# Three PSUM slots for the score tiles of the first two heads, and a load semaphore of their own for queries and keys, in an attention stage

## What is computed

```
qkv = (h @ W_qkv + b_qkv).reshape(b, l, 3, H, D)
q, k, v = (qkv[:, :, 0], qkv[:, :, 1], qkv[:, :, 2])
scores = jnp.einsum('blhd,bmhd->bhlm', q * scale, k)
attn = jax.nn.softmax(scores, axis=-1)
o = jnp.einsum('bhlm,bmhd->blhd', attn, v).reshape(b, l, c)
```

## Time and profile before

| | us |
|---|---|
| median of 3 runs | 3302.26 (3299.76 to 3304.22) |
| the profiled execution | 3293.01 |
| its span from the first to the last instruction | 3291.3 |
| mean granted TensorE clock in it | 0.937 of full speed |
| PE busy in it | 2889.1 (88%) |
| DVE, POOL, ACT busy in it | 1710.2, 1524.9, 1399.2 |

### The profile page before, as it was taken

How to read it: one execution, slowest core, us unless ns; L and a number is a source line. 1 busy time by engine, 2 the same in 40 slices (tenths; PEclk the granted TensorE clock), 3 DMA queues, 4 the chain that set the end, 5 groups by cost and what they waited for, 6 DMA issues and landing times. The chain is left out here.

```text
span 3291.3 us, 49525 instructions
## 1 busy us (share of the span) xinstructions
PE 2889.1 (88%) x16066; PEld 2291.0 (70%) x16066; DVE 1710.2 (52%) x2926; ACT 1399.2 (43%) x1758; POOL 1524.9 (46%) x1144
## 2 busy tenths in 40 slices
PE   6759899967999999999999867649999999999976
PEld 2247777844666666666666556549999999999965
DVE  3446566546888888888888667831111111111125
ACT  2112222215888888898888812211111111111112
POOL 1232322115888888888888848842222222222210
PEclk9869899977999999999999978869999999999988
DMA  5365566561333333333333157567121121111144
GB/s 168 135 228 203 184 212 216 187 176 42 73 80 78 70 80 81 71 76 81 75 73 80 39 175 243 209 225 230 35 69 35 35 69 35 48 56 35 49 138 145
DMA packets 337308, 373.72 MB, mean 114 GB/s; under 512 B 166161, under 2 KB 229273, under 8 KB 337166
## 3 DMA queue, kind: packets, MB, share of 16 engines
q1 hardware_dynamic: 329688, 359.12, 36.7%
q10 hardware_dynamic: 7482, 12.69, 1.3%
HBM read 221.81 MB, written 149.36 MB: 113 GB/s over the span
## 5 line engine op out<-in xcount | busy, mean ns | idle before, releaser
L757 POOL TENSOR_TENSOR a_pl<-a_pf,a_ph 128x1024 fp32r<-128x1024 f32 x384 | 913.1, 2398 | 57.0 <-ACT a_pf L840 56.6
L774 DVE TENSOR_REDUCE a_mx<-a_psum_s 128x1 f32<-128x1024 f32 x512 | 626.0, 1223 | 203.2 <-PE a_psum_s L855 195.1
L838 ACT ACTIVATE a_ph<-a_psum_t 128x1024 fp32r<-128x1024 f32 x512 | 526.1, 1027 | 166.6 <-PE a_psum_t L870 148.0
L1424 POOL TENSOR_TENSOR m_al<-m_af,m_ah 128x256 fp32r<-128x256 f32 x288 | 212.5, 738 | 764.9 <-DVE m_ah L1433 764.9
L1472 PE MATMUL m_psum_h<-m_ht,m_w 128*128 128x256 f32 x4032 | 533.3, 283 | 33.6 <-DMA m_w<-w_s 25.0
L1472 PEld LDWEIGHTS m_psum_h<-m_ht,m_w 128*128 128x128 f32 x4032 | 507.4, 189 | 37.2 <-issue 37.1
L1433 DVE CAST m_ah<-m_af 128x256 fp32r<-128x256 f32 x288 | 84.6, 294 | 837.0 <-ACT m_af L1410 837.0
L1486 PE MATMUL m_psum_y<-m_w,m_ah 128*128 128x288 f32 x2304 | 504.4, 296 | 1.4 <-DVE m_y L1450 1.2
L1410 ACT ACTIVATE m_af<-m_psum_h,m_bias 128x256 f32<-128x256 f32 x288 | 137.3, 477 | 813.4 <-PE m_psum_h L1472 813.4
L887 PE MATMUL a_psum_o<-a_ph,a_vs 128*100 128x512 f32 x1024 | 406.6, 397 | 3.7 <-POOL a_pl L757 3.6
L888 PE MATMUL a_psum_o<-a_pl,a_vs 128*100 128x512 f32 x1024 | 403.9, 394 | 0.0
(11 more groups left out here) (215 smaller groups left out, 3184.8 us busy)
## 6 DMA issues: line engine op xcount, KB each, us to landing
a_qs<-q_s SPq DMA_DIRECT2D x192, 144.0 KB
a_ks<-k_s SPq DMA_DIRECT2D x192, 144.0 KB
w_s<-q_ws SPq DMA_DIRECT2D x64, 324.0 KB, 3.4
h_s<-p_ht SPq DMA_DIRECT2D x40, 512.0 KB, 5.3
m_ht<-h_s SPq DMA_DIRECT2D x16, 1280.0 KB, 8.1
v_s<-q_vo SPq DMA_DIRECT2D x64, 288.0 KB, 2.3
a_vs<-v_s SPq DMA_DIRECT2D x128, 144.0 KB
q_s<-q_qko SPq DMA_DIRECT2D x32, 512.0 KB, 2.7
```

Source lines behind the costliest of these rows:

```text
L757: pool.tensor_tensor(pl[:, s % RING], pf[:, s % RING], raw(ph[:, s % RING]), ALU.subtract).then_inc(lo_pool, 1)
L774: dve.tensor_reduce(mx[:, u % 2, t:t + 1], p_s[:], AX.X, ALU.max).then_inc(s_free, 1)
L838: act.activation(ph[:, s % RING], p_t[:, s % 2], ACT.Exp, scale=SCALE)
L1424: pool.tensor_tensor(al[:, f % RING], af[:, f % RING], raw(ah[:, f % RING]), ALU.subtract).then_inc(lo_ready, 1)
```

## The change

The lead's tiles go round three slots: `p_s` and the two halves of `p_t`, tile n to slot n % 3. PE waits before tile n (from n = 3 on) for the reduction of tile n-3, and no longer for that of tile n-1. The first two scores steps of head 0, which overwrite the halves of `p_t`, wait for the last reductions that read these (`s_free` at 14 and 15). DVE's `turn` of head 0 stands behind the ninth reduction, where it stood behind the eighth.

`loaded[u]` becomes `qk_in[u]` (six DMAs) and `v_in[u]` (two). Score tiles wait for `qk_in`, at the place where they waited for `loaded`. The value product of each head's first step waits for `v_in`, a wait that wasn't there, in all 64 heads. Nothing is computed in another way, and no DMA changes its place.

```diff
-    LOADS = 8
+    QK_LOADS, V_LOADS = 6, 2
+    LEAD = 2 * KT
...
+        lead_slots = (p_s[:], p_t[:, 0], p_t[:, 1])
...
-                                         t[s, bass.ds(hd * D, D), :]).then_inc(loaded[u], 16)
+                                         t[s, bass.ds(hd * D, D), :]).then_inc(qk_in[u], 16)
...
-                          .then_inc(loaded[u], 16)
+                          .then_inc(v_in[u], 16)
...
+                def lead_max(n):
+
+                    dve.wait_ge(s_ready, n + 1)
+                    dve.tensor_reduce(mx[:, n // KT, n % KT:n % KT + 1], lead_slots[n % 3], AX.X, ALU.max) \
+                       .then_inc(s_free, 1)
+
                 def max_tile(hd, u, t):
 
-                    if t == 0 and not (isinstance(hd, int) and hd < 2):
+                    if t == 0:
                         dve.wait_ge(mh_lo, hd - 1)
...
-                for hd in range(2):
-                    for t in range(KT):
-                        max_tile(hd, hd, t)
-                    if hd == 0:
+                for n in range(LEAD):
+                    lead_max(n)
+                    if n == KT:
                         turn(0, 0, None)
...
-                def score_tile(hd, u, i, t):
-
-                    if t == 0:
-                        pe.wait_ge(loaded[u], 16 * LOADS * (i + 1))
-                    if not (isinstance(hd, int) and hd == 0 and t == 0):
-                        pe.wait_ge(s_free, KT * hd + t)
+                def score_product(out, u, t):
+
                     for h in range(L // 512):
-                        m = pe.matmul(p_s[:, h * 512:(h + 1) * 512], qs[0:SROWS, u, t * P:(t + 1) * P],
+                        m = pe.matmul(out[:, h * 512:(h + 1) * 512], qs[0:SROWS, u, t * P:(t + 1) * P],
                                       ks[0:SROWS, u, h * 512:(h + 1) * 512], start=True, stop=True)
                     m.then_inc(s_ready, 1)
+
+                def lead_tile(n):
+                    u, t = divmod(n, KT)
+                    if t == 0:
+                        pe.wait_ge(qk_in[u], 16 * QK_LOADS)
+                    if n >= 3:
+                        pe.wait_ge(s_free, n - 2)
+                    score_product(lead_slots[n % 3], u, t)
+
+                def score_tile(hd, u, i, t):
+
+                    if t == 0:
+                        pe.wait_ge(qk_in[u], 16 * QK_LOADS * (i + 1))
+                    pe.wait_ge(s_free, KT * hd + t)
+                    score_product(p_s, u, t)
...
-                    elif not (isinstance(hd, int) and hd == 0 and s < 2):
+                    elif isinstance(hd, int) and hd == 0 and s < 2:
+                        pe.wait_ge(s_free, LEAD - 2 + s)
+                    else:
                         pe.wait_ge(exp_done, STEPS * hd + s - 1)
...
-                def values(hd, u, s):
+                def values(hd, u, i, s):
 
                     lh, j = divmod(s, PER_LH)
+                    if s == 0:
+                        pe.wait_ge(v_in[u], 16 * V_LOADS * (i + 1))
...
-                for hd in range(2):
-                    for t in range(KT):
-                        score_tile(hd, hd, 0, t)
+                for n in range(LEAD):
+                    lead_tile(n)
```

More of the change, by code:

```diff
@@ L661, in stage_attention @@
         p_o = ps("o", [P, LH, GT])
+        lead_slots = (p_s[:], p_t[:, 0], p_t[:, 1])
         first_set_up, set_up = sem("first_set_up"), sem("set_up")
-        loaded = [sem(f"loaded{i}") for i in range(SLOTS)]
+        qk_in = [sem(f"qk_in{i}") for i in range(SLOTS)]
+        v_in = [sem(f"v_in{i}") for i in range(SLOTS)]
         max_in = [sem(f"max_in{i}") for i in range(SLOTS)]
@@ L846, in _ @@
                 pe.sem_inc(p_free, RING)
+                def score_product(out, u, t):
+                    for h in range(L // 512):
+                        m = pe.matmul(out[:, h * 512:(h + 1) * 512], qs[0:SROWS, u, t * P:(t + 1) * P],
+                                      ks[0:SROWS, u, h * 512:(h + 1) * 512], start=True, stop=True)
+                    m.then_inc(s_ready, 1)
+                def lead_tile(n):
[5 more added lines that the diff above has]
+                    score_product(lead_slots[n % 3], u, t)
                 def score_tile(hd, u, i, t):
                     if t == 0:
-                        pe.wait_ge(loaded[u], 16 * LOADS * (i + 1))
-                    if not (isinstance(hd, int) and hd == 0 and t == 0):
-                        pe.wait_ge(s_free, KT * hd + t)
-                    for h in range(L // 512):
-                        m = pe.matmul(p_s[:, h * 512:(h + 1) * 512], qs[0:SROWS, u, t * P:(t + 1) * P],
-                                      ks[0:SROWS, u, h * 512:(h + 1) * 512], start=True, stop=True)
-                    m.then_inc(s_ready, 1)
+                        pe.wait_ge(qk_in[u], 16 * QK_LOADS * (i + 1))
+                    pe.wait_ge(s_free, KT * hd + t)
+                    score_product(p_s, u, t)
                 def scores(hd, u, i, s):
@@ L903, in body @@
                             scores(hd + 1, (u + 1) % SLOTS, i + (u == SLOTS - 1), s + AHEAD - STEPS)
-                        values(hd, u, s)
+                        values(hd, u, i, s)
                         if not (last and u >= SLOTS - 2):
```

## The result

The changed kernel took 3272.51 us, the median of 6 runs (3268.71 to 3279.80). The ratio is 0.9918, with a 95% interval of 0.9903 to 0.9933: 22 to 32 us faster. In the pair of profiles 24.0 us of the gain lie in the attention stage, where the forecast had put 23.2; what it missed was the time of the kernel before and how much that varies.

The account below looks back on a forecast made before the run. The prediction took the lead's single PSUM slot, with PE and DVE alternating, as the bound. Saving 1.7 us at the start and 21.5 in the lead, 23.2 off the median 3302.26, gave 3279.1 us, range 3274 to 3287.

Parts of the forecast that it names:

- The mechanism: Attention lead, first matmul to first exponential: the single PSUM slot bounds it; with three slots DVE becomes the bound.
- Start of the lead: First lead matmul no longer waits for head 0's values, so PE begins 1.7 us earlier, bounds 1.2 and 2.2.
- Pitch of the lead: Lead reductions on DVE start 1.13 us apart in place of 2.54 a tile; other end 1.25.
- The turn and the maxima: End of lead: turn starts at 737.99, adding 0.24 to later reductions; maxima land at 742.7, before the fourteenth reduction's end, 743.98.
- The wait for values: Added PE wait at each head's first value product, 64 times: taken as costing nothing, 5.8 us at most.
- Rival 2, the clock: PE's clock rises to 2.4 GHz within the lead, making head 0's first steps fast: about 2.0 us more, 3277; chance 0.13.
- The sum: Gain up to the first exponential: 23.2 us, 1.7 from the start and 21.5 from the lead.
- The number: Whole kernel's forecast time on the median: 3279.1 us, range 3274 to 3287.

Follow-up runs that it names:

- more_waits: Changed kernel plus five more already satisfied waits on PE, once a head, at the wait for values; 3269.85 us, ratio 0.9927 to the kernel before.
- slots_only: Against the changed kernel: three slots kept, but one load semaphore as before and no wait for values in the loop; 3275.45 us, ratio 0.9933 to the kernel before.
- four_slots: Against the changed kernel: a fourth lead slot, the PSUM tile of the value products; 3272.08 us.
- again: The changed kernel once more, without edit, beside 17 runs of the kernel before; 3272.47 us, ratio 0.9926.
- two_slots: Against the changed kernel: two PSUM slots in the lead in place of three; 3282.15 us.

## Why the prediction was right or wrong

**The mechanism: right.** One PSUM slot was the bound of the lead, and DVE is now. The slot series (40.26, 22.91, 18.66, 18.66) shows both.

**Start of the lead: right within its bounds.** 1.7 forecast (1.2 to 2.2); 1.9 in the first pair of profiles, 1.5 on the mean of ten and by the packets of the changed kernel's trace.

**Pitch of the lead: right.** 1.13 forecast from instructions of like size in the loop, 1.14 measured over the first three reductions and 1.13 over the next (737.73 - 734.34 = 3.39 for three). The strict reading of the Trainium skill's sentence (VectorE: DVE Perf Modes, "The DRAIN you can't avoid"), 1.23 and more, was not what happened here; the same passage adds that a next operation which is not held starts earlier, which I had left out, and the trace agrees with that. What was off is PE's side: I expected it to wait some 0.3 a tile, and its weight loads mostly wait 0.6.

**The turn and the maxima: right in order, one part too dear.** The turn started 11.46 behind the first matmul (740.00 - 728.54), forecast 11.43. It cost DVE 0.10 and not 0.24: the three reductions from 737.73 on, with the turn among them, take 3.49 (the next group starts at 741.22), where three take 3.39 without it. The scores of head 0 came right behind the fourteenth reduction, as forecast: this starts at 744.61, ends 1.23 later at 745.84, and the scores' first matmul stands at 745.97, where 0.05 had been forecast for the hand-over and 0.13 were needed. Two waits stand there, and the row for such a place was at hand: 0.14 at the ninth tile. The last packets of the maxima stand in 743.5:744, and none in 744:745.5; with the 1.0 that I took behind the last packet they were in by 745.0, ahead of the reduction's end, as forecast. DVE's rows have no gap where head 1's tiles begin, so these were never late. From first matmul to first exponential: 18.66, forecast 745.29 - 726.56 = 18.73.

**The wait for values: right.** Nothing, as taken; the bound of 5.8 was far off. The row that gave it (0.09 at the ninth tile) shows a wait at which PE stands idle, and more_waits shows that with matmuls in flight six waits cost nothing inside the loop's body.

**Rival 2, the clock: right to be kept apart, its price too high.** The clock stayed at 0.50 through the lead of the first profile:

```profile
729.00:747.00 18.00, 18.00 (x34) 8.41 (x33) 17.20 (x17) 0.00 (x0) 0.39 (x2) 0.50 0.62 130
...
756.00:760.00 4.00, 4.00 (x17) 2.54 (x16) 2.52 (x3) 3.48 (x4) 3.60 (x2) 1.00 0.01 2
```

In two of the five executions with three or four slots and no added matmuls it did rise in the lead, and fell again within it (slots_only for 739 to 743, then four_slots for 735 to 741):

```profile
739.00:743.00 4.00, 2.96 (x8) 1.03 (x7) 4.00 (x4) 0.00 (x0) 0.00 (x0) 0.90 0.82 194
```
```profile
735.00:741.00 6.00, 4.12 (x13) 1.67 (x11) 6.00 (x6) 0.00 (x0) 0.00 (x0) 1.00 0.93 203
```

Their leads took 18.66 all the same. The rule of the Trainium skill that I had weighed (TensorE: Matmul & The Clock Gate, "What's actually happening": activity releases the throttle) would have had it rise in the lead; it did in two executions of five, and changed no time there, since DVE sets the pace. The 2.0 us that I gave for it needed full clock in head 0's first steps, and these have gaps of their own.

**The sum: 23.2 forecast, 23.7 in the stage by head 1's turn** (60.40 - 36.71), and 24.0 by the stage's end. Up to the first exponential it was 23.5. Of the rest, 0.2 lies between there and head 1's turn, and 0.3 in the loop (1048.64 and 1048.32, where it took from 1048.2 to 1048.6 in all executions but that of more_waits). Where an execution does differ by more is the clock's return in head 0: measured from the first exponential, it came 8 to 11 us later in all runs, and where it came late (about 11, in again, more_waits and two_slots) the turn of head 2 followed that of head 1 by 18.1 to 18.3 in place of 17.34.

**The number: wrong, by the base and by the range.** Two terms failed, and neither is about the change. First, I took 3302.26, the median of three runs, as the kernel's time. With more runs it was 3300.53 (6), 3294.47 (17) and 3292.45 (9). Those three lay high; 3294.47 - 23.2 = 3271.3, beside 3272.47 measured. Of the 6.6 by which the forecast missed, 1.7 is the step from three runs to six (3302.26 - 3300.53); the other 4.8 is the difference between the 28.0 of that comparison and my 23.2, of which the traces put 0.8 in the attention stage. Second, in "How the numbers follow" the range took in "the spread of the runs below (2.5)". Executions of the kernel before lie from 3287.75 to 3304.49, and in the traces the stages ahead of the attention alone end 9.7 us apart. The profile had said so in one place: the profiled execution stood 9.25 below the median, which I used as a constant to add and not as a sample of the spread. A range of 8 us on either side would have held the result, and the spread of the base asks for one of that size, since the effect was known to 1 us and the base was not. What stays open is why the first comparison gave 28.0 where later ones gave 22.0 and 22.6. The traces allow for it by the spread of the stages around, and part of that goes with the granted clock ahead of the attention. The first three runs have no clock on record, though, so this isn't shown for them, and the two later comparisons ran on different chips, so that a difference by the chip isn't ruled out either. By timing alone the comparisons can't be told apart: their intervals are 22 to 32 and 19 to 30 us.

## What to carry to other kernels

Where two engines alternate over one buffer, the pace is the sum of their latencies (2.54 here). With enough buffers it is the slower engine's start-to-start distance. Read that from neighbours of like size elsewhere in the trace (1.13 here, shorter than the 1.22 that the rows show for one). The number of buffers that is enough is that sum over that distance, rounded up (2.54 / 1.13, so 3), and one more bought nothing. When the effect is worked out to a microsecond, the range is the spread of the base: take it from all executions at hand, the profiled one among them, and compare traces by the stage's own start.

## What the runs showed of the hardware that I had not expected

- The stages ahead of the attention, with identical code, ended between 718.22 and 727.90 in ten executions, while the lead behind them repeated to 0.01 (18.65 and 18.66 in five of them). The granted clock over 0:718 was 0.87 or 0.88 in the three latest and 0.89 in the earliest.
- A short DVE instruction between two long ones costs less than its duration: the turn's 0.20 delayed the reductions behind it by 0.10 (3.49 in place of 3.39 for three).
- Six waits on satisfied semaphores in a row cost PE nothing in the loop's body (17.40 from turn to turn, as before). The loop with five of them more took 0.2 us more at its jump (18.06 in place of 17.83).
- The granted clock fell to 1.2 GHz inside the lead after a stretch at 2.4 in which PE was busy 4.02 of 6.00 us, and not in one in which it was busy 16.95 of 17.00.
